# Attention sums of a graph kernel: three of every sixteen message products move from GpSimd to VectorE

## The reference, cut to what matters

```python
attn = ex / jnp.maximum(denom[dst], 1e-10)
out = jax.ops.segment_sum(h_src * attn[..., None], dst, num_segments=n)
return out.reshape(n, H * D) + bias
```

## Time and profile before

| what | us |
|---|---|
| median of 3 runs (4880.99 to 4883.00) | 4882.64 |
| the profiled execution, its own time | 4879.91 |
| its span, first to last instruction | 4877.9 |
| the stage `attention_sums` in it, first product to last add | 713.15 to 1004.31 |

### The profile page before, as it was taken

The page is one execution under the profiler, slowest core; times in us unless marked ns, Lnnn a source line. Parts: engine busy times, 40 slices in busy tenths (PEclk is TensorE's granted clock), DMA queues, the critical chain, the costliest instruction groups (busy, mean ns, idle before and its releaser), DMA issues. The chain is left out here.

```text
span 4877.9 us, 93729 instructions
## 1 busy us (share of the span) xinstructions
PE 3881.3 (80%) x21956; PEld 3267.0 (67%) x21957; DVE 3015.1 (62%) x7281; ACT 2228.7 (46%) x4904; POOL 2966.6 (61%) x3202
## 2 busy tenths in 40 slices
PE   6999818859999688877788688876888868887598
PEld 4666517758888577766777577775777757777465
DVE  5666676662222466666777666776776766767544
ACT  3222237622222355555555545554555545555221
POOL 3777719813333377765777567774777747776142
PEclk9999959969999899998999899998999989999599
DMA  6888828724565455544555345553555535554332
GB/s 214 253 254 255 244 78 229 206 98 142 181 181 179 141 157 157 157 142 135 156 156 156 121 154 156 157 156 119 156 156 156 156 120 156 156 156 137 128 117 72
DMA packets 391928, 780.24 MB, mean 160 GB/s; under 512 B 175133, under 2 KB 232081, under 8 KB 374568
## 3 DMA queue, kind: packets, MB, share of 16 engines
q0 software_dynamic: 136704, 358.82, 25.8%
q1 hardware_dynamic: 244049, 401.10, 25.4%
q10 hardware_dynamic: 11094, 19.50, 1.2%
HBM read 666.39 MB, written 114.48 MB: 160 GB/s over the span
## 5 line engine op out<-in xcount | busy, mean ns | idle before, releaser
L2163 POOL DMA_INDIRECT g_g<-xl_rows,src_all x1664 | 1581.2, 950 | 536.0 <-issue 453.1
L2188 PE MATMUL g_b<-g_we,g_ea 128*128 128x256 f32 x4160 | 1158.5, 402 | 467.2 <-DVE g_msg L2283 455.1
L2201 PEld LDWEIGHTS g_b<-g_onehot,g_msg 128*128 128x128 f32 x8320 | 1109.5, 197 | 125.8 <-DVE agg L2304 36.1
L2201 PE MATMUL g_b<-g_onehot,g_msg 128*128 128x128 f32 x8320 | 1136.6, 281 | 37.1 <-DVE agg L2304 19.4
L2188 PEld LDWEIGHTS g_b<-g_we,g_ea 128*128 128x128 f32 x4160 | 729.1, 195 | 624.0 <-DVE g_msg L2283 551.7
L2265 ACT ACTIVATE g_msg<-g_msg 128x512 f32<-128x512 f32 x1040 | 652.8, 628 | 827.6 <-DVE g_msg L2283 815.5
L2304 DVE TENSOR_TENSOR agg<-agg,g_b 128x256 f32 x2080 | 866.8, 417 | 258.9 <-issue 136.6
L2283 DVE TENSOR_TENSOR g_msg<-g_g,g_b 128x512 f32<-128x512 f32 x1040 | 710.7, 683 | 493.4 <-DMA g_g<-xl_rows,src_all 326.4
L2245 ACT ACTIVATE g_away<-iota_row,dst_rel 128x128 f32<-128x128 f32 x1040 | 405.9, 390 | 224.7 <-DMA g_g<-xl_table,src_all 148.0
L2163 POOL DMA_INDIRECT g_g<-xl_table,src_all x416 | 395.7, 951 | 168.2 <-issue 114.6
L513 POOL DMA_INDIRECT sc_g<-h_table,sc_idx x416 | 406.9, 978 | 132.2 <-issue 116.4
(11 more groups left out here) (321 smaller groups left out, 4110.0 us busy)
## 6 DMA issues: line engine op xcount, KB each, us to landing
g_ea<-in_ea SPq DMA_DIRECT2D x260, 512.0 KB
ex_w<-in_f_w SPq DMA_DIRECT2D x80, 1024.0 KB, 6.4
e_rows<-sc_g SPq DMA_DIRECT2D x52, 1088.0 KB, 5.0
at_g<-e_rows SPq DMA_DIRECT2D x104, 544.0 KB, 4.5
g_g<-xl_rows,src_all POOLq DMA_INDIRECT x1664, 2.8
sc_rel<-rel_row ACTq DMA_DIRECT2D x52, 256.0 KB, 5.1
xl_rows<-g_rows SPq DMA_DIRECT2D x20, 640.0 KB, 3.3
sc_g<-h_table,sc_idx POOLq DMA_INDIRECT x416, 4.8
```

The costliest lines, as they stand in the source:

```text
L2163: nc.gpsimd.indirect_dma_start(out=g.g[:, j, 0:width], out_offset=None, in_=table[:, :], in_offset=bass.IndirectOffsetOnAxis(ap=k.src_all[ ...
L2188: last = nc.tensor.matmul(ep[u % EB][:, i * D:(i + 1) * D], g.ea[:, q, (at + i) * P:(at + i + 1) * P], g.we[:], start=True, stop=True)
L2201: last = nc.tensor.matmul(ps[u % (SB // 2)][:, at:at + P], g.msg[:, j, b * P:(b + 1) * P], g.onehot[:, j, :], start=True, stop=True)
```

## The change

Of every round's 16 products, GpSimd keeps 13. Tiles 4, 9 and 14 (`BY_DVE`) are weighted by VectorE, by the same `tensor_tensor`, placed between its adds three places ahead of the tile (`V_AHEAD`): at places 1, 6 and 11 of the round. They count on a semaphore of their own, `by_dve`; `weighted` now counts 13 a round. TensorE and SP wait for `by_dve` as well as for `weighted` where the pair, or the quads so far, hold such a tile. VectorE's loop takes two rounds a turn, with the first two rounds written out, because the product names the half of `attn` by a constant. SP's loop over rounds is written out for all 25 rounds. The diff, cut to its core:

```diff
+    BY_DVE = (4, 9, 14)
+    ON_POOL = BODY - len(BY_DVE)
+    V_AHEAD = 3
+    def of_pool(j):
+        return j - sum(t < j for t in BY_DVE)
+    def of_dve(j):
+        return sum(t < j for t in BY_DVE)
...
-            with sp.Fori(0, ITERS // ROUNDS - 1) as turn:
-                for r in range(ROUNDS):
-                    it = turn * ROUNDS + r
-                    for v in range(QUADS):
-                        sp.wait_ge(weighted, it * BODY + 4 * (v + 1))
-                        load_rows(v, it + 1)
...
+            for it in range(ITERS - 1):
+                for v in range(QUADS):
+                    sp.wait_ge(weighted, it * ON_POOL + of_pool(4 * (v + 1)))
+                    if of_dve(4 * (v + 1)):
+                        sp.wait_ge(by_dve, it * len(BY_DVE) + of_dve(4 * (v + 1)))
+                    load_rows(v, it + 1)
+                    if v % 2 == 1 and it + ROUNDS < ITERS:
+                        load_attn(it % ROUNDS, v // 2, it + ROUNDS)
...
-                        product(r, j).then_inc(weighted, 1)
+                        if j not in BY_DVE:
+                            product(nc.gpsimd, r, j).then_inc(weighted, 1)
...
-                    pe.wait_ge(weighted, it * BODY + 2 * u + 2)
+                    pe.wait_ge(weighted, it * ON_POOL + of_pool(2 * u + 2))
+                    if 2 * u in BY_DVE or 2 * u + 1 in BY_DVE:
+                        pe.wait_ge(by_dve, it * len(BY_DVE) + of_dve(2 * u + 2))
...
-            def body(it, first):
+            def weight_tile(turn, r, j):
+                it = turn * ROUNDS + r
+                dve.wait_ge(rows_in[j // 4], it * 16 + 16)
+                dve.wait_ge(attn_in[2 * r + j // HALF], turn * 16 + 16)
+                dve.wait_ge(summed, it * BODY + j - j % 2 + 2)
+                product(nc.vector, r, j).then_inc(by_dve, 1)
+            def body(turn, r, first):
+                it = turn * ROUNDS + r
                 bases = lagging_bases(k, dve, base_regs, it * BODY)
                 for j in range(BODY):
+                    if j + V_AHEAD in BY_DVE:
+                        weight_tile(turn, r, j + V_AHEAD)
                     if j >= LAG or not first:
                         add_tile(it * BODY + j - LAG, (j - LAG) % BODY, bases[j])
-            body(0, True)
-            with dve.Fori(1, ITERS) as it:
-                body(it, False)
+            for r in range(ROUNDS):
+                body(0, r, r == 0)
+            with dve.Fori(1, ITERS // ROUNDS) as turn:
+                for r in range(ROUNDS):
+                    body(turn, r, False)
```

More of the change, by code:

```diff
@@ L859, in attention_sums @@
         attn_in = [sem(f"attn_in{n}") for n in range(2 * ROUNDS)]
-        weighted, unit, distance, hot, summed, added = map(sem, (
-            "weighted", "unit", "distance", "hot", "summed", "added"))
+        weighted, by_dve, unit, distance, hot, summed, added = map(sem, (
+            "weighted", "by_dve", "unit", "distance", "hot", "summed", "added"))
         block = c.enter_context(nc.Block())
@@ L866, in rows_of, with product @@
             return k.e_rows[bass.ds(it, 1), :, 4 * v:4 * v + 4, :].rearrange("a p t c -> p (a t) c")
-        def product(r, j):
-            return nc.gpsimd.tensor_tensor(
+        def product(engine, r, j):
+            return engine.tensor_tensor(
                 msg[:, j, :].rearrange("p (h c) -> p h c", h=HEADS), head_cols(g[:, j, 0:HROW]),
```

## The result

The changed kernel takes 4894.66 us (median of 8 runs, 4884.95 to 4898.09); the kernel before, in the same set, 4881.44 (one of its eight runs took 9832.04 and counts in no ratio). The ratio is 1.0026 [1.0015, 1.0038], some 13 us slower, against a forecast of 4898.

A forecast was written before the change was run, and what follows sets the result against it. VectorE's chain of adds and head reads was taken as the bound. Products +7.2, waits behind GpSimd +11.7 and heads -3.3 sum to +15.6 us: 4879.9 becomes 4895.5, and 4898 for the median, 2.7 above; range 4884 to 4930.

The forecast's parts named there:

- The bound: VectorE's chain of adds and head reads sets the stage's round, 11.09 us; GpSimd waits, idling 1.67 us a round.
- Products on VectorE: 78 products between VectorE's adds widen the spacing by 0.12, 0.12 and 0.05 us, 0.29 a round: +7.2 us.
- the gain of the first round: VectorE's waits for messages in the first round, 0.8 us at best, set off against +0.6 of spacing: nothing.
- GpSimd beside it: VectorE's products wait for GpSimd's running SBUF product, 0.15 us each, 78 times: +11.7 us, bounds 0 and 36.
- Heads: Two rounds a turn in VectorE's loop remove 13 of 24 jumps, each head from 1.88 to 1.63: -3.3 us.
- New waits: VectorE's, TensorE's and SP's added waits should not bind; sequencer steps 0 to 0.2 us a product, taken as 0.
- (a): Rival: VectorE's products slip into GpSimd's gaps and never meet its runs, +3.9 us, 4886.5; chance 0.27.
- (b): Rival: no gap between GpSimd's products, so VectorE waits for the end of a run, +77 us, 4960; chance 0.10.
- The mark: Sign for rival (b): a VectorE product taking longer than 0.33 + 0.46 us.
- (c): Rival: GpSimd is the bound and VectorE's head waits for messages, -35 us, 4848; chance 0.07 with its relative.
- (d): Rival: VectorE starves for TensorE's lead or rows, some tenths of a microsecond a product, inside the range; no separate chance.

The follow-up runs named there:

- in pairs: Kernel before, with a round's 16 bases read two at a time between the adds of a pair instead of all at the head: ratio 1.0089, stage 325.8 us.
- one read a turn: Changed kernel's loops with no product on VectorE, the 32 bases of two rounds read at once instead of 16 a round: ratio 0.9991, stage 291.3 us.
- the kernel in which GpSimd reads nothing: Changed kernel with GpSimd's 13 products a round replaced by memsets of zeros that read no SBUF: ratio 1.0001 (one run), stage 299.3 us.
- loops alone: Changed kernel with `BY_DVE` empty, so GpSimd weights all 16 tiles and only the rewritten loops of VectorE and SP remain: ratio 0.9992, stage 291.3 us.
- the kernel with all products at the head: Changed kernel with VectorE's three products of a round all placed ahead of the reading of the bases, not between adds: ratio 1.0029, stage 312.4 us.
- the two sums: Kernel before, with odd tiles added into a second sum, merged at the end: ratio 0.9903, stage 245.8 + 7.1 us; the same on the changed kernel: 0.9867.
- two sums and two products: Changed kernel with two sums and two products a round on VectorE (tiles 9 and 14) instead of three: ratio 0.9876, stage 227.2 + 7.1 us.

## Why the prediction was right

**The bound.** Right. With 3.3 us of rest a round for GpSimd the stage grew by what VectorE was given. The reading of the heads is shown by the bases read elsewhere: in pairs, 1.88 became 0.38; with one read a turn the second head became 0.13 at the same round.

**Products on VectorE:** predicted 7.2 us, measured 7.9 (the kernel in which GpSimd reads nothing, less loops alone). The term was drawn from a product between two dependent adds, 0.67 us apart in the earlier trace rows; the 72 of the steady rounds in the kernel whose GpSimd reads nothing are 0.674 apart, against 0.554 in a pair and 0.622 between pairs without a product, which makes 7.0. What I had not foreseen is one add in every turn, the same each time, that comes 0.11 late (a gap of 0.31 instead of 0.20; 0.55 the first time, at 750.55 above): another 1.6 us in the steady rounds, of which 0.6 comes back, since the second add behind each product starts 0.01 sooner. It is there in both of these kernels with VectorE products and not in loops alone; its cause was not found. In the first 28 adds the products cost nothing: the spacings there, heads left out, sum up to 17.25 us with them and 17.44 without, since fewer adds wait for messages (of which GpSimd has fewer to make and, in this kernel, shorter ones). That is the gain of the first round that I had put at nothing.

**GpSimd beside it:** predicted 11.7, measured 10.4. The shut time is right almost to the digit: I took 0.15 us before the recorded end from a single pair of rows, and it is 0.14. The Trainium skill (SBUF — State Buffer, Who interferes with whom) has the second instruction blocked until the first is finished; by these rows it goes on 0.14 sooner, and so ahead of the next product of GpSimd's run. Off was the share of the time in which GpSimd works: I took 0.8 for all three places (the 0.65 worked out ahead of it is 0.64). By place the products took 0.62, 0.60 and 0.44 us: tiles 4 and 9 wait 0.20 and 0.18, as much as with GpSimd always at work, but at tile 14's place GpSimd mostly rests for rows, as at 742.74, and that product waits 0.02. That the mean, 0.13, comes so near to my 0.15 is partly luck: no place has it. GpSimd's own products lengthen by up to 0.27 (881 ns), 34 of them; that costs nothing beside its rests.

**Heads:** predicted -3.3, measured -4.4 with all that belongs to the loops. The mis-sized quantity is the head without a jump, 1.52 and not 1.63: the heads gave 5.0 (13 x 0.36 and 0.3 at the first). Against them the adds of the first two rounds took 1.0 more (I had set +0.6 off against -0.8), and the first add came 0.4 us sooner after the first load.

**New waits:** rightly nothing, as far as the steady rounds go; loads and TensorE wait for VectorE, but VectorE for neither. The steps of the sequencer are hidden where a product stands between two adds; ahead of the reading, where nothing hides them, they cost the 0.2 us a product that the prediction gave as their upper bound.

So 7.9 + 10.4 - 4.4 = 13.9, where 7.2 + 11.7 - 3.3 = 15.6 was forecast; the errors are +0.7, -1.3 and -1.1.

**The rivals.** (a), the products in the gaps, would have been the kernel in which GpSimd reads nothing, 299.3 us; it holds for tile 14 alone. (b), no gap, falls: the longest product is 0.89 us, a wait of 0.47, which is still less than one GpSimd product less 0.14 (0.48), so no wait in the changed kernel reached past the running instruction into the next. What the rival describes did happen once elsewhere, at 723.79 in the kernel with all products at the head. The mark that the prediction set for it, 0.33 + 0.46, was wrong: 0.33 is the spacing of independent instructions, and a product's recorded time begins at 0.42, so the mark had to be 0.88 or, with the measured 0.14, 0.90. (c), GpSimd as the bound, falls by the direction alone, and its condition is shown by the two sums: there GpSimd is the bound, and the same edit takes 17 us off. (d), starving, falls with the heads, which are those of loops alone.

## What to carry to other kernels

Before work is moved to an engine that looks less busy, find the one that is late: here the engine with 175 us of work set the pace and the one with 242 us waited, and the same edit was worth +13 us, or -17 once a second sum had broken the chain of dependent adds. VectorE and GpSimd products, each of two SBUF tiles, kept each other out here, so the price of such a move is, as a rule, part of one engine's instruction for each meeting of the two; keep them apart in time, and not back to back. Break the dependence first, then share out the work.

## What was not expected of the hardware

- Adds that wait for the one before start 0.55 to 0.62 apart; adds that wait for the last but one, 0.33, with 0.42 recorded for each. Doing away with the wait for the predecessor took 45 us off this program, with 7.1 us of closing add in it.
- A read of bases into registers runs beside products that are already queued on the same engine (a head of 2.18 with 2.33 of products in it, 1.52 without any), but it starts 0.6 later, once the sequencer is through the waits of three products; and a small read between two adds is not hidden (0.55 to 0.88).
- In 245 of 246 waits a VectorE product stood behind one GpSimd product, for 0.52 us at most; once it stood behind seven, for 3.70 us.
- TensorE's granted clock, from 760 to 920, was 0.90 in the mean (of stretches at its two levels, 2.4 and 1.2 GHz) in the changed kernel, where TensorE waits for VectorE's products and is busy 120.41 of 160 us, 0.96 in the kernel before with 131.31, and 1.00 with two sums and two products with 154.59; its matmuls took 300, 292 and 283 ns. That cost nothing here, as TensorE was not late. The rows of the kernel before and of the changed one:

```profile
760.00:920.00 160.00, 131.31 (x919) 116.01 (x920) 97.90 (x233) 108.00 (x287) 139.37 (x239) 0.96 0.80 216
760.00:920.00 160.00, 120.41 (x880) 113.30 (x881) 109.09 (x265) 102.16 (x271) 108.94 (x180) 0.90 0.71 197
```
